# A power operation on GpSimd in place of eight VectorE steps for the reciprocal standard deviation of a GNN layer

## The reference

```python
h = jnp.maximum(_layernorm(x, axis=-1), 0.0)
agg = jax.ops.segment_sum(edge_attr, i, num_segments=x.shape[0])   # i = src
t = jnp.concatenate([h, agg], axis=-1)
t = jax.nn.silu(t @ W1 + b1)
t = t @ W2 + b2
mu = jnp.mean(t, axis=-1, keepdims=True)
var = jnp.mean(jnp.square(t - mu), axis=-1, keepdims=True)
t = (t - mu) * jax.lax.rsqrt(var + LN_EPS) * ln_gamma + ln_beta
out = x + (t + h)
```

## Time and profile before

| | us |
|---|---|
| median of three runs | 728.91 (728.89 to 729.11) |
| span of the profiled execution | 769.9 |
| VectorE busy in it | 713.3 |
| TensorE busy in it (modelled ends) | 711.9 |
| ScalarE busy in it | 629.7 |
| GpSimd busy in it | 490.1 |

### The profile page before, as it was taken

How to read it: one execution, slowest core, us unless ns; L and a number is a source line. 1 busy time by engine, 2 the same in 40 slices (tenths; PEclk the granted TensorE clock), 3 DMA queues, 4 the chain that set the end, 5 groups by cost and what they waited for, 6 DMA issues and landing times.

```text
span 769.9 us, 15386 instructions
## 1 busy us (share of the span) xinstructions
PE 711.9 (92%) x4554; PEld 592.7 (77%) x4554; DVE 713.3 (93%) x2275; ACT 629.7 (82%) x2034; POOL 490.1 (64%) x414
## 2 busy tenths in 40 slices
PE   7999998689999999999999999999999999999994
PEld 3555546578888888888888888888888888888883
DVE  8999997889999999999999999999999999999888
ACT  7999985478878787878787888787879788879793
POOL 3000017577878777778777777777777777777730
PEclk9999999799999999999999999999999999999997
DMA  5000000123333333333333333333323233322112
GB/s 203 1 2 1 2 3 23 46 76 105 104 103 105 104 104 103 106 105 103 105 105 101 104 102 105 103 105 102 107 100 112 96 107 102 108 90 81 49 65 78
DMA packets 28265, 65.89 MB, mean 86 GB/s; under 512 B 8473, under 2 KB 10028, under 8 KB 28180
## 3 DMA queue, kind: packets, MB, share of 16 engines
q1 hardware_dynamic: 15604, 51.90, 18.6%
q0 software_dynamic: 12576, 12.99, 7.0%
HBM read 52.05 MB, written 25.60 MB: 101 GB/s over the span
## 4 chain that ended last, share of the span: by engine, by line
DVE 43%; PE 22%; issue 20%; another core or an unknown queue 6%; ACT 6%; DVEq 0%
DVE stat L824 9%; DVE R L1031 7%; DVE R L1006 6%; PE za L702 6%; DVE lo L1024 5%; DVE T L1036 4%; PE y L658 4%; ACT hi L549 4%; PE za L653 2%; PE pre L653 2%; PE za L646 2%; PE za L687 2%; PE pre L646 2%; DVE guess_off L879 1%
## 5 line engine op out<-in xcount | busy, mean ns | idle before, releaser
L436 POOL DMA_INDIRECT G<-in_edge_attr_dram,slot_edge x388 | 479.9, 1237 | 144.0 <-issue 123.2
L741 PEld LDWEIGHTS y<-w2c,S 128*128 128x128 f32 (+1 forms) x1556 | 189.9, 193 | 9.4 <-issue 1.4
L741 PE MATMUL y<-w2c,S 128*128 128x128 f32 (+1 forms) x1556 | 191.0, 276 | 1.3 <-ACT S L556 1.3
L539 ACT ACTIVATE H<-X,shift,rstd 128x128 f32<-128x128 f32 x392 | 163.4, 508 | 2.7 <-issue 2.7
L716 PE MATMUL pre<-hi,w1h 128*128 128x512 f32 (+1 forms) x392 | 163.4, 417 | 1.9 <-issue 1.2
L1024 DVE TENSOR_TENSOR lo<-za,hi 128x1024 fp32r<-128x1024 f32 (+1 forms) x98 | 119.4, 1218 | 42.3 <-ACT hi L549 35.7
L717 PE MATMUL pre<-hi,w1l 128*128 128x512 f32 (+1 forms) x392 | 154.6, 394 | 0.0
L556 ACT ACTIVATE S<-pre,b1c 128x512 f32<-128x512 f32 (+1 forms) x196 | 127.4, 723 | 8.2 <-remote 4.7
L721 PE MATMUL pre<-lo,w1h 128*128 128x512 f32 (+1 forms) x392 | 122.8, 394 | 0.1
L824 DVE BATCH_NORM_STATS2 stat<-X 128x6 f32<-128x128 f32 x392 | 107.6, 285 | 0.1
L702 PE MATMUL za<-HOT,G 128*128 128x128 f32 (+1 forms) x784 | 105.1, 277 | 2.3 <-issue 1.6
(11 more groups left out here) (154 smaller groups left out, 990.3 us busy)
## 6 DMA issues: line engine op xcount, KB each, us to landing
X<-in_x_dram SPq DMA_DIRECT2D x48, 512.0 KB
out_dram<-R SPq DMA_DIRECT2D x48, 512.0 KB
G<-in_edge_attr_dram,slot_edge POOLq DMA_INDIRECT x388
X<-in_x_dram SPq DMA_DIRECT2D x1, 424.0 KB
out_dram<-R SPq DMA_DIRECT2D x2, 192.0 KB
w1f<-in_L_gnn_W_dram SPq DMA_DIRECT2D x1, 256.0 KB, 2.7
w2f<-in_L_gnn_W_dram SPq DMA_DIRECT2D x1, 128.0 KB, 2.7
srci<-in_src_dram SPq DMA_DIRECT2D x1, 85.8 KB
```

The source lines that it names most:

```text
L436: nc.gpsimd.indirect_dma_start(G[b.j][:, t, :], None, source, bass.IndirectOffsetOnAxis(ap=slot_edge[:, bass.ds(b.number(TILES, t), 1)], a ...
L539: done = nc.scalar.activation(H0[b.j][:, t, :], X[b.xj][:, t, :], ACT.Relu, bias=shift[b.j][:, t:t + 1], scale=rstd[b.ring(POWERS_LAG)][:, ...
L741: done = nc.tensor.matmul(places[t][0:r], S[c][:, m, t * r:(t + 1) * r], w2c[:, m, :], start=False, stop=True, skip_group_check=True)
```

## The change

The eight steps from the seed to `rstd` leave VectorE's `powers`. In their place GpSimd does one `tensor_tensor` with the operation `pow`, of `var` and a constant tile of -0.5, in the middle of each block's gathers: after the fifth of them, and by itself where no gathers are left. It waits for `var_done` from VectorE and signals `rstd_done`, on which VectorE waits before `shift`. The residual and the eight statistics, which stood between the steps, now stand one after another between `var` and that wait. The eighth gather is paced by the statistics (`bn_done`) in place of a step. `last_powers` stays as it is.

```diff
-    SMALLS = 11
-    STATISTICS_AT = {1: (0,), 2: (1,), 3: (2,), 4: (3,), 5: (4,), 6: (5,), 8: (6,), 9: (7,)}
+    SMALLS = 2
...
+            nc.gpsimd.memset(minus_half[:], -0.5)
...
-                else:
-                    at_least(pool, small, b.plus(3).number(SMALLS, 9))
+                elif b.plus(4).exists(NB):
+                    at_least(pool, bn_done, b.number(1, 5))
+
+            def powers_of(b):
+
+                pool.wait_ge(var_done, b.number(1, 1))
+                nc.gpsimd.tensor_tensor(out=rstd[b.ring(POWERS_LAG)][:], in0=var[:], in1=minus_half[:],
+                                        op=ALU.pow).then_inc(rstd_done, 1)
...
                     if pacer is not None:
+                        if c and t == HALF + 1:
+                            powers_of(pacer.plus(3))
                         pace(pacer, c, t - c * HALF)
...
                 gather(Block(0), 1, source, limit)
+                powers_of(Block(1))
                 for c in range(2):
                     gather(Block(1), c, source, limit)
...
                 def step(b):
+                    if b.is_number(0):
+                        powers_of(Block(2))
                     if b.plus(2).exists(NB):
                         for c in range(2):
                             gather(b.plus(2), c, source, limit, pacer=b)
+                    else:
+                        powers_of(b.plus(3))
...
             gather_first(edge_limit)
+            powers_of(Block(0))
...
-                    if b.plus(1).exists(NB) and b.n > 3:
-                        for t in STATISTICS_AT.get(place, ()):
-                            statistics(b.plus(1), t)
-                    if b.plus(-3).exists(NB):
-                        if place == 1:
-                            x_plus_beta(b.plus(-3))
-                        if place == 2:
-                            residual(b.plus(-3))
+                    if b.plus(-3).exists(NB) and place == 1:
+                        x_plus_beta(b.plus(-3))
...
-                link_small(nc.vector.tensor_scalar(out=guess[0][:].bitcast(I32), in0=var[:].bitcast(I32), scalar1=-0.5,
-                                                   scalar2=float(RSQRT_SEED), op0=ALU.mult, op1=ALU.add))
...
-                link_small(nc.vector.scalar_tensor_tensor(out=rstd[b.ring(POWERS_LAG)][:], in0=guess_sq[:], scalar=1.875,
-                                                          in1=guess[1][:], op0=ALU.add, op1=ALU.mult))
+                nc.vector.scalar_tensor_tensor(out=var[:, 0:TILES], in0=m2[:], scalar=1.0 / D, in1=mdd[:],
+                                               op0=ALU.mult, op1=ALU.add).then_inc(var_done, 1)
+                if b.plus(-3).exists(NB):
+                    residual(b.plus(-3))
+                if b.plus(1).exists(NB) and b.n > 3:
+                    for t in range(TILES):
+                        statistics(b.plus(1), t)
+                dve.wait_ge(rstd_done, b.number(1, 1))
                 nc.vector.scalar_tensor_tensor(out=shift[b.j][:], in0=msum[:], scalar=-0.5, in1=rstd[b.ring(POWERS_LAG)][:, 0:TILES],
                                                op0=ALU.mult, op1=ALU.mult).then_inc(powers_done, 1)
```

## The result

The changed kernel takes 875.63 us (median; 872.87 to 876.31) against 729.01 us for the kernel before beside it (728.89 to 729.19): 1.2005 times the time, 95% interval 1.199 to 1.2019. It is 147 us slower, and the forecast of 759 us (710 to 800) had the sign right and the size wrong.

What follows compares the result with a forecast made beforehand. VectorE's chain was taken to bound the kernel before; afterwards GpSimd's block, 8 x 1.30 + 0.30 + 0.30 + 1.0 + 1.0 = 13.0 us. With +4 at start and tail: 741 or 778, middle 759 us, range 710 to 800.

Steps and rivals of the forecast that it cites:

- the 12.82 us block: Steady block of the kernel before, 500 / 39 in the first profile, which GpSimd's block would exceed by 0.2 us.
- the 0.67 and 0.76 us waits: Per block, TensorE's turning of h waits 0.67 for VectorE's `lo`, and `lo` waits 0.76 for ScalarE's `hi`.
- The full queue: GpSimd's gathers in the kernel before: 64% busy, but busy and idle time together fill the whole 12.80 us block.
- The 0.14 us of room: GpSimd's spare time per block before the change: 2.84 idle seen less 2.70 fixed.
- X: Cost of the power operation on GpSimd per block: taken as 1.0 us, from 0.16 to 1.6.
- second semaphore and issue ahead of the power: Idle time in GpSimd's block: 0.30 for a second semaphore wait plus 0.30 in front of the power.
- B: Stretching of GpSimd's gathers beside VectorE operations reading two SBUF operands: 1.97 us per block before, 1.0 after (0.3 to 2.0).
- my two readings: Profile against timed runs: all shrinks alike (0.947), 741 us; or timed blocks run without VectorE's waits, 778 us.
- The rival by which VectorE's saving is eaten by its own wait: VectorE's wait for `rstd` exceeds 0.87 us per block although GpSimd has room; no chance of its own.
- VectorE's saving: Eight steps leave VectorE, 0.87 us less per block, from 12.0 to 11.1 us.
- the dear power: Rival: power on GpSimd of 1.6 us and more, GpSimd's block 13.6, time 805 us and up; chance 0.10.
- the first rival: Cheap power on GpSimd, 0.2 us, its block 12.2, level with TensorE: 706 us (700 to 726); chance 0.20.

Runs made afterwards that it cites:

- the unused power: Kernel before, its eight VectorE steps kept, plus a GpSimd power of constants after each block's fifth gather that nobody reads: 838.19 us, 1.1497 times before.

## Why the prediction was wrong

**Bound.** Right in kind: the chain of the changed kernel is GpSimd's, its idle time before gathers stayed at 0.30, `shift` waits for `rstd`. Wrong in what it rested on: the 12.82 us block, and the 0.67 and 0.76 us waits in it, belonged to that one execution. So is a reading: the 26.3 us ahead of the turning hold 3.6 of "issue", and the wait for `lo` is 22.7, 0.58 per block. The full queue was half an illusion too. With 11.98 us per block the mean gather of the kernel before took 1.15 us, not the 1.246 of the earlier trace rows, and with six gathers a block it took 1.29 and the time did not change: the stretching seems to fill what the block leaves, though no run tested that by itself. The 0.14 us of room were too few as well, since the unused power of 2.94 us lengthened the block by 2.28.

**X, the step that failed.** I wrote X = 1.0, from 0.16 to 1.6. It is 2.93. I named it a routine and then priced it by the only routine in view, a gather, whose 1.00 us says nothing of a price per column; and the upper end, eight plain operations, assumed that the power costs no more than what it replaces. The sum, term by term, against the timeline of the result:

- eight gathers with idle time: 10.40 taken; 8.00 + 7 x 0.30 + 0.19 + 0.03 = 10.32 measured;
- second semaphore and issue ahead of the power: 0.60 taken; nothing beyond the line above was there;
- B: 1.0 taken, 9.54 - 8.00 = 1.54 measured, the gather of 2.13 us at the beta add alone 1.13 (the mean gather of 1.1 us that was to show B is 1.188);
- X: 1.0 taken, 2.93 measured.

13.0 becomes 14.8, and of the difference of 1.8 X is +1.93, B +0.54 and the gaps -0.68. That B and the gaps nearly cancel is luck; X alone makes the miss. With 2.93 for X alone, the second of my two readings gives 45 x (1.0 + 1.93) + 4 = 136 and 865 us, the first 823. That X decides is also what the experiments say: product 735.79, eight columns 810.52, sixteen 875.63.

The price that the Trainium skill (GPSIMD Engine Reference, section 3.1) leads to for a two-input add, an estimate of 0.03 us beside the dispatch, is well under the 0.23 that the product took with its dispatch, and says nothing of a power. Its section 4.1 advises against two-input elementwise work on GpSimd; the runs agree, at 1.2005 times for the power and 1.0057 for the product.

**B and the lock.** The rule that I cited from the Trainium skill (SBUF — State Buffer, "SBUF: two separate sides"), by which a power would wait for the residual's end, is borne out, where VectorE's operation starts first, in the tail of the changed kernel:

```profile
848.30 1.22 DVE L1031 TENSOR_TENSOR R<-H,R 128x1024 f32<-128x1024 f32 x1
852.35 0.17 DVE L884 SCALAR_TENSOR_TENSOR shift<-msum,rstd 128x8 f32<-128x8 f32 x1 [2.83 <-POOL rstd L433]
```

```profile
848.47 3.85 POOL L433 TENSOR_TENSOR rstd<-var,minus_half 128x16 f32<-128x16 f32 x1 [3.36 <-DVE var L876]
```

The power lasts 3.85 us instead of 2.93: it starts 0.17 after the residual and ends at 852.32, 2.8 to 2.9 after the residual does (near 849.5). In the steady block the power comes when the residual is over, so there the wait cost nothing. The other way round the rule does not show. By it, whichever of the two starts first blocks the other; but in the run with the unused power 57 of the two-operand sums `R<-T,R` lie wholly within a power that had started before them. They last 0.681 us in the mean, against 0.683 for the other 39, and start no later behind the instruction before them.

**Cover.** "In latency that is enough for an operation of up to about 2 us" was right, 2.77 less what the residual holds up, and the operation took 2.93. The rival by which VectorE's saving is eaten by its own wait was put at the dear power's end and is real: 1.27 us per block with six gathers.

**Start and tail.** Start: +2.9 for the first `rstd` was 4.7 (116.12 in the earlier trace rows, 120.86 now: X again), and up to the first beta add it is 12.7, not 4.9, because the powers of the next blocks stand in series with the gathers behind them: GpSimd waits 3.89 us for `var` of block 1 and is 2.94 us busy with its power before the first gather of block 1, at 135.86. Tail: a gain of 0.46 per block became a loss; from the residual's end to `shift` pass 2.8 to 2.9 us, against 1.66 for the eight steps.

**VectorE's saving.** Of the 0.87 us per block the run with the product and six gathers shows 0.77 in VectorE's busy time (457.37 us in blocks of 11.98 against 433.25 in blocks of 11.83). It is worth 0.15 at most, since no version here has a steady block under 11.83. So the first rival, a cheap power at 706 us, was not to be had either: with a product and the queue as it is the kernel came to 735.79, with room to 720.67.

**The two readings.** The second was right: blocks run without the waits take 11.98 us. I had the evidence (idle time of 37 us against 41 missing) and took the middle.

## What to carry to other kernels

Before an operation is moved to an engine whose queue is in the steady chain, time it alone at its real width; a name such as "one power" says nothing of its price, and an upper bound must not be taken from what it replaces. When a profiled span is 5% off the timed median, take a second profile before any wait in it is priced. A busy share near 100% with modelled ends is no floor, and one near 70% is no room: take work away from each engine in turn and see which of them moves the time.

## What the runs showed of the hardware

The power on GpSimd takes 0.70 us for one column on 128 partitions and 5.43 for 32, some 0.15 per column; a product of 16 columns takes 0.23 in the mean of its run, and 0.46 in the mean of the run with six gathers. Behind an elementwise operation the next gather starts after 0.15 to 0.19 us, where behind a gather it takes 0.30, and an elementwise operation that need not wait starts 0.02 to 0.03 after a gather. A gather that starts within 0.11 us of the start of a VectorE operation with two SBUF operands lasts 1.98 to 2.13 us instead of 1.00, and a power that starts 0.17 us into one lasts 3.85 instead of 2.93. A power that is already running did not hold up VectorE's two-operand sums, 0.681 us against 0.683.
